# Setup of a two-layer graph kernel: dense adjacency built from the highest targets down, spill list made between rounds

## The reference

```python
deg_out = segment_sum(w, s, n)
deg_in = segment_sum(w, d, n)                      # self loops included
wn = w * rsqrt(deg_out)[s] * rsqrt(deg_in)[d]
def step(h, _):                                    # ten times
    agg = segment_sum(h[s] * wn[:, None], d, n)
    return 0.9 * agg + 0.1 * feat, None
x = layernorm(x + h)
x = layernorm(x + attention_over_edges(x, edge_attr, src, dst))
```

## Time and profile before

| | |
|---|---|
| median of 3 runs | 9977.31 us (9974.46 to 9978.49) |
| profiled execution, time | 9976.81 us |
| its span | 9975.0 us |
| first GpSimd gather of the run part (L1646) | starts at 1642.59 us |
| PE busy in the span | 8829.3 us (89%) |
| POOL busy in the span | 7255.4 us (73%) |
| zeroes written to `dense`, five transfers of 26112 KB, one of 44800, one of 6400 | 186 MB |
| first node rows, from issue to landing | 17.6 us |

### The profile page before, as it was taken

One profiled execution on the slowest core, in us unless ns is written; L12 is line 12 of the kernel. 1 busy time (PEld: TensorE's weight loads), 2 busy tenths in 40 slices (PEclk: granted clock), 3 DMA queues, 4 the chain that ended last, 5 costly groups with the idle time before them and its releaser, 6 DMA issues.

```text
span 9975.0 us, 144406 instructions
## 1 busy us (share of the span) xinstructions
PE 8829.3 (89%) x50368; PEld 4786.6 (48%) x50368; DVE 4943.6 (50%) x14438; ACT 5539.0 (56%) x7215; POOL 7255.4 (73%) x7701
## 2 busy tenths in 40 slices
PE   3999997999999999999999999999999766666666
PEld 2777774333333333333333333333333465655665
DVE  7666663443444434444344443444434455566666
ACT  1333334787777777777777777777777411111111
POOL 5677776777777777777777777777777377777776
PEclk5555556999999999999999999999999777777676
DMA  9972225999999999899999999999999565555554
GB/s 359 394 279 64 74 71 174 347 344 310 347 310 347 339 317 347 309 346 334 323 347 309 347 326 331 348 308 348 318 336 342 167 162 143 143 145 143 143 143 119
DMA packets 1378005, 2669.54 MB, mean 268 GB/s; under 512 B 683776, under 2 KB 713379, under 8 KB 1377270
## 3 DMA queue, kind: packets, MB, share of 16 engines
q1 hardware_dynamic: 958006, 2245.72, 63.3%
q0 software_dynamic: 248000, 261.74, 10.7%
q10 hardware_dynamic: 171264, 152.74, 5.3%
HBM read 2426.96 MB, written 232.42 MB: 267 GB/s over the span
## 4 chain that ended last, share of the span: by engine, by line
PE 42%; POOL 39%; issue 14%; DMA 3%; DVE 2%; ACT 1%; SPq 0%; POOLq 0%; DVEq 0%; ACTq 0%
PE banks L2369 25%; POOL arena L1646 23%; POOL arena L1660 15%; PE banks L2330 10%; PE banks L2420 3%; PE banks L2332 3%; DMA arena<-node_rows,src_idx 1%; PE banks L2413 1%; DMA x_sb<-in_edge_weight_dram 1%; PE banks L2447 1%; DMA u_sb<-key_rows 1%; DMA arena<-dense 0%; POOL dense L1622 0%; DVE arena L1934 0%; POOL arena L1642 0%
## 5 line engine op out<-in xcount | busy, mean ns | idle before, releaser
L1646 POOL DMA_INDIRECT arena<-node_rows,src_idx x4800 | 4582.3, 955 | 1583.8 <-issue 1452.0
L1716 ACT ACTIVATE arena<-arena 128x1024 f32<-128x1024 f32 x4900 | 4762.2, 1044 | 1380.2 <-DMA arena<-dense 1224.3
L2369 PE MATMUL banks<-arena 128*64 128x512 f32 x12240 | 2715.0, 595 | 19.8 <-ACT arena L1716 19.5
L2369 PE MATMUL banks<-arena,u_sb 128*64 128x512 f32 x11760 | 2613.1, 596 | 82.3 <-ACT arena L1716 82.0
L1660 POOL DMA_INDIRECT arena<-kv_rows,src_idx x1568 | 1503.1, 959 | 597.2 <-issue 477.7
L2103 DVE TENSOR_SCALAR arena<-banks,rel,w_tab 128x128 f32<-128x128 f32 x4800 | 1603.5, 403 | 123.2 <-DVE arena L2120 99.6
L2369 PEld LDWEIGHTS banks<-arena 128*64 128x64 f32 x12240 | 877.0, 138 | 1544.4 <-issue 1467.8
L2369 PEld LDWEIGHTS banks<-arena,u_sb 128*64 128x64 f32 x11760 | 844.4, 138 | 1552.3 <-issue 1467.6
L2330 PE MATMUL banks<-arena 128*128 128x98 f32 x3136 | 1174.7, 478 | 93.0 <-ACT arena L1695 92.9
L1622 POOL DMA_INDIRECT dense<-arena x1012 | 980.4, 969 | 370.8 <-issue 314.6
L1765 ACT ACTIVATE banks<-arena 128x64 f32<-128x64 f32 x196 | 44.6, 228 | 1694.6 <-DVEq L2248 1694.6
(11 more groups left out here) (241 smaller groups left out, 6399.4 us busy)
## 6 DMA issues: line engine op xcount, KB each, us to landing
arena<-dense SPq DMA_DIRECT2D x3550, 512.0 KB
dense<-blank SPq DMA_DIRECT2D x5, 26112.0 KB, 189.5
arena<-in_dst_dram SPq DMA_DIRECT2D x195, 512.0 KB
arena<-node_rows,src_idx POOLq DMA_INDIRECT x4800
arena<-in_edge_attr_dram SPq DMA_DIRECT2D x195, 256.0 KB, 3.2
u_sb<-key_rows ACTq DMA_DIRECT2D x26, 1792.0 KB
dense<-blank SPq DMA_DIRECT2D x1, 44800.0 KB, 195.0
arena<-key_rows ACTq DMA_DIRECT2D x23, 1792.0 KB
```

Source lines behind the costliest of these rows:

```text
L1646: gp.indirect_dma_start(out=rows_in[:, n % ROWS, s, :], out_offset=None, in_=node_rows[k % 2], in_offset=bass.IndirectOffsetOnAxis(ap=src_ ...
L1716: nc.scalar.activation(planes[:, q % PLANES, half, :], ring[:, n % SLOTS, :], ACT.Relu, scale=-1.0 if half else 1.0).then_inc(planes_act, 1)
L2369: done = mm(banks[h * D:(h + 1) * D, sum_slot(k, g), :], u, rows[:, h * 512:(h + 1) * 512], start=first, stop=last, tile_position=(0, h * ...
```

## The change

The chunks of high targets are cut smaller and all rounds run in another order: folded chunks from the highest targets to the lowest, then chunk 0 (additions), then chunk 1 (sums). Zeros are written in this order in half groups of 512 columns, with a semaphore each; GpSimd waits at a chunk's start for the halves that the chunk touches. The special narrow transfer of the first 128 columns goes. The signs are computed before round 0, the digits in rounds 0 to 2, the checks in rounds 6 to 20. One-hot batches begin in round 4 and are paced 2 per round against 3 in chunk 0 (in units of 196/557 batch). The spill list is counted in round 236, placed in round 241 and named in round 246 instead of after the last round; GpSimd fetches spilled edges 12 rounds before its end. TensorE does all eight L2330 multiplies of a batch and then all eight L2332 ones.

```diff
-CHUNKS = [(19, 0), (16, 2), (36, 1), (36, 1), (33, 1), (33, 1), (33, 1), (33, 1), (33, 1)]
+CHUNKS = [(19, 0), (16, 2), (36, 1), (36, 1), (36, 1), (36, 1), (33, 1), (15, 1), (14, 1), (13, 1), (11, 1), (7, 1)]
-FETCH_AT = 8
+FETCH_AT = 12
+HOT_FROM = 3
...
-    ROUND_OF = [(c, i) for c, (n, near) in enumerate(CHUNKS) for i in range(n)]
+    CHUNK_ORDER = list(range(len(CHUNKS) - 1, SUM_CHUNKS - 1, -1)) + list(range(SUM_CHUNKS))
+    ROUND_OF = [(c, i) for c in CHUNK_ORDER for i in range(CHUNKS[c][0])]
+    FOLD_ROUNDS = sum(n for n, near in CHUNKS[SUM_CHUNKS:])
...
+    COUNTED_AT, PLACE_AT, NAME_AT = 16, FOLD_ROUNDS + 4, FOLD_ROUNDS + 9
+    PACE = [3 if c == 0 else 2 for c, i in ROUND_OF]
     def hots_upto(rnd):
-        return max(0, rnd + 1 - CHUNKS[0][0]) * HOT_BATCHES // (ROUNDS - CHUNKS[0][0])
+        return sum(PACE[HOT_FROM:rnd + 1]) * HOT_BATCHES // sum(PACE[HOT_FROM:])
...
-        clear(sp, 0, 0, FIRST_COLS).then_inc(first_cleared, 16)
-        sp.wait_ge(rows_loaded[0], 32)
-        for g in range(GROUPS):
-            clear(sp, g, 0 if g else FIRST_COLS, WIDTH[g]).then_inc(dense_cleared[g], 16)
+        clear(sp, GROUPS - 1, GROUP // 2, GROUP).then_inc(dense_cleared[GROUPS - 1][1], 16)
+        sp.wait_ge(rows_loaded[0], 16)
+        clear(sp, GROUPS - 1, 0, GROUP // 2).then_inc(dense_cleared[GROUPS - 1][0], 16)
+        for g in range(GROUPS - 2, 0, -1):
+            clear(sp, g, GROUP // 2, GROUP).then_inc(dense_cleared[g][1], 16)
+            clear(sp, g, 0, GROUP // 2).then_inc(dense_cleared[g][0], 16)
+        clear(sp, 0, 0, GROUP).then_inc(dense_cleared[0][0], 16)
...
-                top = BASE[(CHUNK_AT[c] + CHUNKS[c][0] * STREAMS) // 2 - 1] + P - 1
-                pool.wait_ge(first_cleared, 32)
-                for g in range(top // GROUP + 1 if top >= FIRST_COLS else 0):
-                    pool.wait_ge(dense_cleared[g], 16)
+                low = BASE[CHUNK_AT[c] // 2]
+                top = BASE[(CHUNK_AT[c] + CHUNKS[c][0] * STREAMS - 1) // 2] + P - 1
+                pool.wait_ge(first_cleared, 16)
+                for g in range(low // GROUP, top // GROUP + 1):
+                    for h, z in enumerate(dense_cleared[g]):
+                        if not g or low < g * GROUP + (h + 1) * GROUP // 2 and top >= g * GROUP + h * GROUP // 2:
+                            pool.wait_ge(z, 16)
...
+            if rnd == 0:
+                src_digits()
             if rnd == 1:
-                signs()
+                dst_digits()
             if rnd == 2:
+                dst_steps()
+            if rnd == 6:
                 count_outside()
...
+            if rnd == FOLD_ROUNDS - 1:
+                count_spill()
+            if rnd == PLACE_AT:
+                place_spill()
+            if rnd == NAME_AT:
+                name_spill()
...
             for t in range(HB):
-                col = n * HB + t
-                s0 = BASE[col // 2] // QUART
-                end = n == HOT_BATCHES - 1
                 mm(banks[:, 4, 0:NB], hot_lo[:, n % 2, t, :], hot_hw[:, n % 2, t, 0:NB], start=False, stop=end and t == HB - 1, skip_group_check=True)
+            for t in range(HB):
+                s0 = BASE[(n * HB + t) // 2] // QUART
                 at = t % 4 * QUART
                 last = mm(banks[at:at + QUART, 5, s0:s0 + SPAN], hot_dst[:, n % 2, t, :], hot_hw[:, n % 2, t, NB:NB + SPAN],
```

More of the change, by code:

```diff
@@ L39 @@
 GROUP = 1024
-FIRST_COLS = 128
 TPI = 6
@@ L1246, in fast @@
     first_cleared = sem("first_cleared")
-    dense_cleared = [sem(f"dense_cleared{g}") for g in range(GROUPS)]
+    dense_cleared = [[sem(f"dense_cleared{g}_{h}") for h in range(2 if g else 1)] for g in range(GROUPS)]
     fold_vec = sem("fold_vec")
@@ L1881, in count_far @@
             far = DENSE_TILES - FAR
[L1882 to L1883 removed]
+            link(v.tensor_tensor(src_f[:, 0:far], dst_f[:, 0:far], dst_f[:, FAR:DENSE_TILES], ALU.is_equal))
+            link(v.tensor_reduce(bad[:, 2:3], src_f[:, 0:far], AX, ALU.add))
         def count_near(reach):
@@ L1947, in setup_dve @@
             size, near = CHUNKS[c]
-            keys, weights = row_in[load]
+            keys, weights = row_in[load % 2]
             if not near:
@@ L2085, in setup_dve @@
         dve.wait_ge(tables, 16 * 16)
-        for g in range(GROUPS):
-            dve.wait_ge(dense_cleared[g], 16)
+        for halves_cleared in dense_cleared:
+            for z in halves_cleared:
+                dve.wait_ge(z, 16)
         for z in added:
@@ L2315, in setup_pe @@
                 n += 1
-        pe.wait_ge(bad_counted, 1)
-        nc.tensor.matmul(banks[0:1, 6, 0:1], bad[:, 6:7], ones[:, 0:1], start=True, stop=True).then_inc(bad_summed, 1)
         mm = nc.tensor.matmul
@@ L2324, in setup_pe @@
         for n in range(HOT_BATCHES):
+            if n == hots_upto(COUNTED_AT):
+                pe.wait_ge(bad_counted, 1)
+                mm(banks[0:1, 6, 0:1], bad[:, 6:7], ones[:, 0:1], start=True, stop=True, skip_group_check=True).then_inc(bad_summed, 1)
+            if n == hots_upto(FOLD_ROUNDS - 1):
+                pe.wait_ge(spill_counted, 1)
+                mm(banks[:, 6, 0:1], earlier, spill_count[:, 0:1], start=True, stop=True, skip_group_check=True)
+                mm(banks[0:1, 6, 8:10], ones[:, 0:1], spill_count[:, 0:2], start=True, stop=True, skip_group_check=True).then_inc(spill_based, 1)
+            if n == hots_upto(PLACE_AT):
+                pe.wait_ge(spill_hots, 1)
+                for b in range(SPILL):
+                    for i in range(8):
+                        last = mm(banks[:, 6, 16 + 4 * b:16 + 4 * b + 3], spill_hot[b][:, i, :], spill_at[:, i, :], start=i == 0, stop=i == 7, skip_group_check=True)
+                last.then_inc(spill_listed, 1)
+            end = n == HOT_BATCHES - 1
             pe.wait_ge(hots_scaled, n + 1)
             for t in range(HB):
-                col = n * HB + t
-                s0 = BASE[col // 2] // QUART
-                end = n == HOT_BATCHES - 1
                 mm(banks[:, 4, 0:NB], hot_lo[:, n % 2, t, :], hot_hw[:, n % 2, t, 0:NB], start=False, stop=end and t == HB - 1, skip_group_check=True)
+            for t in range(HB):
+                s0 = BASE[(n * HB + t) // 2] // QUART
                 at = t % 4 * QUART
@@ L2342, in setup_pe @@
         last.then_inc(deg_turned, 1)
-        pe.wait_ge(spill_counted, 1)
-        mm(banks[:, 6, 0:1], earlier, spill_count[:, 0:1], start=True, stop=True, skip_group_check=True)
-        mm(banks[0:1, 6, 8:10], ones[:, 0:1], spill_count[:, 0:2], start=True, stop=True, skip_group_check=True).then_inc(spill_based, 1)
-        pe.wait_ge(spill_hots, 1)
-        for b in range(SPILL):
-            for i in range(8):
-                last = mm(banks[:, 6, 16 + 4 * b:16 + 4 * b + 3], spill_hot[b][:, i, :], spill_at[:, i, :], start=i == 0, stop=i == 7, skip_group_check=True)
-        last.then_inc(spill_listed, 1)
     def run_pe(pe):
```

134 lines of the change are left out of this document (63 added, 71 removed).

## The result

The kernel after takes 9855.32 us (median of 4 executions, 9852.8 to 9858.67), 0.9877 of the kernel before [0.9864, 0.989]: 122 us less. Forecast was 9897 with a range from 9870, so the gain was larger than the range allowed. Its profiled execution took 9852.8 us (span 9851.0), against 9976.8.

The account below looks back on a forecast made before the run. GpSimd's chain of indirect writes was taken to set the flag's time. Its terms were summed to a first gather at 1562.3 us, 80.3 earlier, so 9977.3 - 80 = 9897 us, with a range of 9870 to 9945.

Parts of the forecast that it names:

- The run part: From the first gather on: the diff leaves it alone, so only the time of the flag, 1642.59 us before, counts.
- Start: Setup up to GpSimd's first write: round 0 at 52 us, first signal at 76 us, 23 later than before.
- Plain writes: GpSimd's folded rounds: 948 writes at 1.292 us, 1224.8 us, plus 9 us of early stalls and 2.1 of drain.
- Zeros in time: Zeroing of half groups ahead of GpSimd's writes: 46 us each, no wait, the tightest cover 14 us.
- Additions: GpSimd's 76 additions, now after the plain writes: 145 us taken, between 141 and 151, against 203 before.
- Rival (1): GpSimd's additions stay slow at 2.67 us from their round trip, not the zeros: + 58 us, 9955; chance 0.13.
- Sums: GpSimd's 64 sums, last after the additions: 1.292 us each, 82.7 us.
- Fetches: GpSimd's six fetches of spilled edges: 14.2 us stays, one of 7.47 and five of 1.27.
- TensorE and VectorE: Setup batches: 4.6 to 6.5 us; even at 7.04 landed node rows come at 1519, inside GpSimd's chain by 42 us.
- Rival (2): VectorE and TensorE bind the setup: matters from 7.25 us a batch; at 7.4, 9925 us; chance 0.08.
- Spill list: End of the setup: made in rounds 236 to 246, hidden by VectorE's lead, so GpSimd's 26.9 us wait goes.
- Range: Whole kernel: 9870 to 9945 us, taking in most of (1) in partial form and (2); the forecast's own range 9872 to 9922.

Follow-up runs that it names:

- e5: The kernel before with one plain indirect write of 128 zeros to trash ahead of the first addition, waited for at once: 9949.6 us, 0.9973.
- e7: The kernel after with 52 MB of zeros in 2 KB pieces sent to a scratch tensor while it adds: 9882.88 us, 0.9904.
- e1c: The kernel after with the 128-row and 32-column multiplies of a batch alternating again, as before the change: 9884.7 us, 0.9901.
- e2c: The kernel after with alternating multiplies and the whole spill list made after the last round, on a slow chip (all kernels 12.4 to 12.6 ms): 0.9912.
- e2d: The kernel after with alternating multiplies and the spill list after the last round, a second time, again on a slow chip: 0.9911.
- e3: The kernel before with the grouped order alone, all eight L2330 multiplies of a batch, then all eight L2332 ones, on a slow chip: 0.9932.
- e4: The kernel before with five unused semaphores, which renumbers those of the DMAs, on a slow chip: 0.9995.
- f1: The kernel before with one more short memset near the start of GpSimd's program, on a slow chip: 0.9995.
- f3: The kernel before with three more short memsets near the start of GpSimd's program, on a slow chip: 0.9992.
- g1: The kernel before with one more wait on GpSimd, for VectorE's constants, ahead of the first indirect DMA: 9981.43 us, 1.0.
- e9: The kernel before with an extra indirect DMA that adds 128 zeros to trash ahead of the first addition, on a slow chip: 0.9975.

## Why the prediction was wrong

Measured by its own steps:

- *The run part.* The step that failed is "the diff leaves the run part alone, so the question is when the flag comes". The diff does, but every gather and plain write of GpSimd became 11 ns shorter (an addition 7, by the medians) and the run part 27.3 us. This is 27.3 of the 43.7 us by which the profiled execution lies below its forecast (9896.5), and with it the forecast would have been 9869. e5 showed it apart from the rest of the change (21.8 us of it). Why the DMAs got shorter stays open.
- *Start.* 76 us forecast, 74.43 measured; round 0 at 51.03 us, for 52. Right.
- *Plain writes.* 1224.8 and 9 of stalls and a drain of 2.1: 1235.9. Measured from the first write to the first addition: 1235.6. The sum is right by luck, for its parts are not: GpSimd waits for VectorE only 2.1 us in all of it, near the lower bound of the stalls, but the 948 writes come after 1.302 us on the mean, where the median is 1.263. The 36 us between mean and median are two things that the sum did not have as terms: 13.8 us of DMAs that are busy longer than 0.96 us, beside VectorE's operations (last section), and 22.8 us in six gaps about 143 us apart or twice that, as this one, which end in nothing the profile shows:

```profile
1077.44 0.96 POOL L1631 DMA_INDIRECT dense<-arena  x1 [5.49 <-issue]
```

  The price of 1.292, a mean of the kernel before, held such gaps already; the lengthened DMAs it did not hold, and the 11 ns that each write became shorter made up for them.
- *Zeros in time.* Right: no wait for a cleared half group shows.
- *Additions.* 145 and a drain of 2.1, measured 1310.00 to 1452.34: 142.3, 4.8 less. I took a value between the ends where the row that is nearest to a quiet DMA, 1.55 + 0.30, was the answer (mean 1.848). Rival (1) put the whole of 2.67 on the round trip; it is refuted, since in quiet the same round trip costs no wait and 1.85 is all. The prediction's own reason, the zeros, is a part of it only: 0.23 of 0.70 us from one addition to the next (e7).
- *Sums* 80.9 us for 82.7, *spilled writes and step* 5.1 for 5.4.
- *Fetches.* 14.2 carried over from before, 7.6 measured. The 7.47 us fetch is gone from here, because it was no property of the fetch (next section).
- The terms as I wrote them add up to 1561.3, not 1562.3. This 1.0, 1.9 (start to first addition), 4.8, 1.8, 6.6 and 0.3 make the 16.4 us by which the setup was better than forecast.
- *TensorE and VectorE.* A batch of 4.6 us was forecast from the rows and 4.2 measured; the multiply with 98 moving columns came out at 0.23 (for 0.219), the one with 32-column weights at 0.03 (for 0.070, which was taken from multiplies that move 98 columns; these move 5). That they would cover was right, and TensorE has nothing to do from 1180 us on, 366 us ahead of the first gather. That at 7.04 TensorE would end inside the chain at no cost was wrong: e1c ends it at the forecast time, and it costs 20 to 24 us in the setup, by waits that go with the traffic of its loads. Rival (2) had its point of decision at 7.25 us a batch; the cost begins below it.
- *Spill list.* Right: no wait at L1620. e2c and e2d bring it back, but on slow chips.
- *Range.* Its lower end, 9870, was made from bounds of the setup alone, and not even to their end: additions at 141, no stall and 948 writes at 1.27 are 4, 9 and 21 us less, 9863. With nothing for a part that the diff doesn't touch, it could not hold 9855.

## What to carry to other kernels

Work that only "covers" has a second price: its transfers. When one engine is made faster and stops earlier, look at what its loads ran beside (here the waited-for additions), before calling it worth nothing. A stretch of code that a diff leaves alone can still change by 1% of an instruction's time, and with 6400 such instructions on or near the path that is more than a term of the sum: give a range room for it, and compare that instruction's median in both traces first. A single odd duration in the trace (7.47 us among DMAs of 0.97) should be looked up on the other engines before it is carried over.

## What the runs showed of the hardware

**Indirect DMAs of GpSimd come in two levels.** By the medians, gathers are busy 955 or 958 ns in before, e3, e4, f1, f3 and g1, and 944 to 947 in the kernel after, all its variants, e5 and e9. It holds for a whole execution, for plain writes too (969 to 972, 958 to 962), but not for additions (1548 or 1549 in the first group, 1541 or 1542 in the kernel after and its variants, 1550 and 1552 in e9 and e5). The 3 ns inside a level are another thing: in the executions with 958 or 947 ns a plain GpSimd instruction of the setup (L1591, an affine select) takes 240 or 241 ns for 238, so the whole engine is a little slower there. The 11 ns between the levels don't show there: 238 ns in before and in the kernel after. What sets it stays open: semaphore numbers, program length, the form of the first DMA and the two-semaphore wait ahead of it are excluded one by one. What the kernels with 944 share is that the first indirect DMA is not the addition of round 0, with which the kernel before begins; where it reads from, its own waits, and the three instructions ahead of it in e5 and e9 were not taken apart.

**A long VectorE operation holds up a DMA that GpSimd issues.** In the kernel after one write of GpSimd is busy 6.29 us:

```profile
1179.24 6.29 POOL L1631 DMA_INDIRECT dense<-arena  x1 [0.31 <-issue]
1185.83 0.96 POOL L1631 DMA_INDIRECT dense<-arena  x1 [0.30 <-issue]
```

and VectorE in that time:

```profile
1177.95 6.74 DVE L2088 TENSOR_TENSOR u_sb<-x_sb,inv_out 128x6272 f32<-128x6272 f32 x1
```

VectorE ends at 1184.69, the write at 1185.53, 0.84 later. In the kernel before, the fetch of 7.47 us ends at 1595.16, 0.83 after the same operation (6.68 us from 1587.65) ends. It is so in all twenty traces: a DMA of GpSimd that started 0.04 to 4 us after this operation ends 0.81 to 0.88 us after its end. The write that started 0.02 us after VectorE's operation in the kernel after was not held up (0.96 us). Shorter operations do it too: in the kernel after 17 more writes are busy 1.15 to 2.5 us, and 16 of them end 0.82 or 0.83 us after a VectorE operation of 0.6 us or more. This is why the long fetch left the end of the setup: the operation did not get cheaper, it now meets a plain write at 1179 us and costs the chain 5.3 us there. The Trainium skill, page SBUF — State Buffer, SBUF: two separate sides, says that VectorE and GpSimd share a port pair, and that a VectorE operation with two SBUF inputs holds it for the whole instruction against a GpSimd operation that reads SBUF, if it starts first. This operation has two inputs, and the trace agrees, other than for the write that started 0.02 us after it.

**Additions depend on what else moves.** 1.85 us from one to the next with 0 GB/s beside them (after), 2.08 at 358 GB/s of zeros (e7), 2.6 at 167 to 245 GB/s with loads of rows among it (e1c from 1410 us on; VectorE works there too, and the addition itself is busy 0.04 to 0.11 us longer). So the kind of traffic seems to count, not its rate alone. Why, no run here shows.
